# Filler products for TensorE: the unit matrix times itself in front of waits of a twelve-part decoder kernel

## The reference

```python
x = x + _L0_attn_ref(_layernorm(x), ...)       # first attention: 16 heads in pairs, p1 - lam * p2
x = x + _L0_xattn_ref(ctx_1024, _layernorm(x)) # warping: dynamic time warping against ctx
x = x + _L0_ffn_ref(_layernorm(x), ...)        # trees: 16 leaves, for q, k and v
x = x + _L1_attn_ref(_layernorm(x), ...)       # attention
x = x + _L1_xattn_ref(_layernorm(x), ctx, ...) # memory attention, gated
x = x + _L1_ffn_ref(_layernorm(x), ...)        # first mixture: shared expert + best 2 of 8
x = x + _L2_attn_ref(_layernorm(x), ...)       # pooling: running weighted sums
x = x + _L2_xattn_ref(_layernorm(x), ctx, ...) # attention to ctx
x = x + _L2_ffn_ref(_layernorm(x), ...)        # ternary weights
x = x + _L3_attn_ref(_layernorm(x), ...)       # attention with bias
x = x + _L3_xattn_ref(_layernorm(x), ctx, ...) # attention to ctx
x = x + _L3_ffn_ref(_layernorm(x), ...)        # second mixture: best 2 of 8, a limit per expert
```

```python
# first attention
attn = softmax(einsum('bhqd,bhkd->bhqk', q, k)).reshape(b, H, 2, n, n)
o = einsum('bhqk,bhkd->bhqd', attn[:, :, 0] - lam * attn[:, :, 1], v)
o = (o - mean(o)) * rsqrt(var(o) + 1e-5) * ln_g + ln_b      # per head
return o @ Wo
# memory attention
v_pool = concatenate([normed, memory], axis=1)
attn = softmax(where(mask, (normed @ q_w.T) @ (v_pool @ k_w.T).T * scale, -inf))
return (1 - alpha) * h + alpha * (attn @ v_pool)            # alpha = sigmoid(h @ gate_w.T + gate_b)
# pooling
qw = softmax((query @ Wqa + bqa) / sqrt(D)); pooled_query = cumsum(qw * query) / arange(1, S + 1)
mixed = pooled_query * keys
kw = softmax((mixed @ Wka + bka) / sqrt(D)); pooled_keys = cumsum(kw * mixed) / arange(1, S + 1)
return pooled_keys * values
# both mixtures: a token's two best experts, its place among the expert's tokens, and
y = gelu(x_of_expert @ w1[e] + b1[e]) @ w2[e] + b2[e]       # summed with the two gates
```

## Time and profile before

| | |
|---|---|
| median of 3 runs | 2319.32 us (2319.03 to 2327.06) |
| span of the profiled execution | 2356.9 us, 37.6 us (1.6%) above the median |
| TensorE busy in that span | 1774.8 us (75%), weight loads 1215.4 |
| VectorE, ScalarE, GpSimd busy | 1337.8 us (57%), 1099.5 (47%), 746.9 (32%) |
| first attention | 11.8 to 250.5 us, granted clock 0.85 in its loop (38.0 to 250.5) |
| memory attention | 908.2 to 1043.7 us, granted clock 0.81 |
| first mixture | 1045.8 to 1315.7 us, granted clock 0.91 |
| pooling | 1316.7 to 1453.1 us, granted clock 0.81 |
| second mixture | 2061.1 to 2351.2 us, granted clock 0.76 |

### The profile page before, as it was taken

How to read it: one execution, slowest core, us unless ns; L and a number is a source line. 1 busy time by engine, 2 the same in 40 slices (tenths; PEclk the granted TensorE clock), 3 DMA queues, 4 the chain that set the end, 5 groups by cost and what they waited for, 6 DMA issues and landing times. The chain is left out here.

```text
span 2356.9 us, 39525 instructions
## 1 busy us (share of the span) xinstructions
PE 1774.8 (75%) x14484; PEld 1215.4 (52%) x14484; DVE 1337.8 (57%) x3646; ACT 1099.5 (47%) x2273; POOL 746.9 (32%) x718
## 2 busy tenths in 40 slices
PE   3887553999895996767999386887788868743994
PEld 1555432435543664644798253565555535542774
DVE  3897587502123774654343365885369969862223
ACT  4775531223243775733344243774357657610441
POOL 1223201360354331146255002330223232165453
PEclk9888885798896998877999697998979969955997
DMA  4111361125623301102376200000000010011224
GB/s 158 83 83 82 104 235 45 49 75 150 161 70 132 124 2 50 37 30 85 110 238 201 75 1 27 28 20 10 3 1 2 2 37 28 11 49 60 62 81 138
DMA packets 145170, 173.18 MB, mean 73 GB/s; under 512 B 21073, under 2 KB 120593, under 8 KB 144049
## 3 DMA queue, kind: packets, MB, share of 16 engines
q1 hardware_dynamic: 125252, 129.09, 17.7%
q0 software_dynamic: 13248, 28.21, 3.6%
q10 hardware_dynamic: 6480, 13.37, 1.5%
HBM read 126.84 MB, written 79.05 MB: 87 GB/s over the span
## 5 line engine op out<-in xcount | busy, mean ns | idle before, releaser
L1154 PE MATMUL a_AV<-a_vx,a_pT 128*64 128x18 f32 (+1 forms) x3072 | 115.1, 224 | 33.0 <-DVE a_two L824 15.3
L1154 PEld LDWEIGHTS a_AV<-a_vx,a_pT 128*64 128x64 f32 x3072 | 105.9, 146 | 62.2 <-issue 28.6
L1016 ACT ACTIVATE a_e<-a_e 128x512 f32<-128x512 f32 x192 | 110.2, 622 | 58.7 <-DVE a_e L846 58.5
L1141 PE MATMUL a_TP<-ident,a_e 128*128 128x128 f32 x768 | 108.0, 285 | 20.0 <-ACT a_e L1016 19.4
L1021 ACT COPY a_pT<-a_TP 128x512 f32<-128x512 f32 x192 | 103.4, 588 | 39.6 <-PE a_TP L1141 39.4
L846 DVE TENSOR_TENSOR a_e<-a_S,a_mx 128x1024 f32<-128x1024 f32 x96 | 117.3, 1222 | 2.9
L1141 PEld LDWEIGHTS a_TP<-ident,a_e 128*128 128x128 f32 x768 | 89.2, 146 | 57.6 <-ACT a_e L1016 48.3
L1130 PE MATMUL a_S<-a_kbd,a_qT 64*64 64x512 f32 x768 | 113.8, 668 | 0.9 <-issue 0.6
L3620 POOL DMA_INDIRECT f_back<-f_ys,f_row x78 | 74.7, 957 | 97.5 <-DVE f_ys L3709 85.6
L3126 POOL DMA_INDIRECT f_back<-f_ys,f_row x80 | 76.6, 957 | 87.1 <-DVE f_ys L3287 66.9
L3759 ACT ACTIVATE f_h<-f_H,f_wt 128x256 f32<-128x256 f32 x156 | 65.2, 473 | 83.5 <-PE f_H L3835 83.5
(11 more groups left out here) (544 smaller groups left out, 4731.4 us busy)
## 6 DMA issues: line engine op xcount, KB each, us to landing
f_wt<-in_f_ew SPq DMA_DIRECT2D x39, 584.0 KB
f_slots<-in_blank SPq DMA_DIRECT2D x1, 18576.0 KB
f_wt<-in_f_leaf SPq DMA_DIRECT2D x94, 98.0 KB, 2.0
f_xs<-f_slots SPq DMA_DIRECT2D x47, 144.0 KB
memory_x_k<-w_stage ACTq DMA_DIRECT2D x24, 256.0 KB, 3.2
f_slots<-in_blank SPq DMA_DIRECT2D x1, 5760.0 KB
f_xs<-leaf_slots SPq DMA_DIRECT2D x22, 256.0 KB
leaf_out<-f_ys SPq DMA_DIRECT2D x22, 256.0 KB
```

The source lines that it names most:

```text
L1016: act.activation(eh, eh, ACT.Exp).then_inc(weights.sem, 1)
L1141: last = pe.transpose(TP[:, half, P * n:P * n + P], ev[:, 4 * half + n, :], k.ident[:, :])
L1154: last = pe.matmul(AV[64 * c:64 * c + 64, 2 * hp * W1:2 * (hp + 1) * W1], pT[:, hp, 64 * c:64 * c + 64], vx[:, g % 2, t, c, 2 * hp:2 * hp ...
```

## The change

A helper is added that multiplies the unit matrix (128 x 128, float32) by itself into a PSUM bank, n times, and its calls are put into TensorE's programs. No result of these products is read. 310 products are added: 8 x 4 in first attention, 8 x (5 + 5) in memory attention, 8 x 3 in pooling, 14 + 30 in the first mixture, 130 in the second (10 ahead of `turn_x(0)`, 5 behind it, and in each of the 8 batches 5 before `turn_x(b + 1)`, 5 behind it where there is one, and 5 behind `place(b)`). Nothing is removed. In first attention a wait comes with them: for the semaphore of the copy pT of tile i - 1, since TP is its bank.

```diff
+def keep_warm(pe, k, bank, n):
+
+    for _ in range(n):
+        pe.matmul(bank[:, 0:P], k.ident[:, :], k.ident[:, :], start=True, stop=True)
@@ first attention
                 early(g, t)
+                if i and t == 1 and diff:
+                    pe.wait_ge(pT_half.sem, 2 * (i - 1) + 1)
+                    keep_warm(pe, k, TP[:, 0, :], 4)
                 turn(i)
@@ memory attention
             def weigh(g):
                 if g:
                     pe.wait_ge(values_taken.sem, values_taken.after(g - 1))
+                keep_warm(pe, k, AV[:, 0, :], 5)
                 for t in range(GT):
...
                     weigh(i - 1)
+                if within(i - 1):
+                    keep_warm(pe, k, TP[:, 0, :], 5)
                 if within(i + 1):
                     project(i + 1)
@@ pooling
                     turn_q(i + 1)
+                    keep_warm(pe, k, QKV[:, 0, :], 3)
                 if within(i - 1):
                     total(i - 1, 1, C, (tail_ready.sem, tail_ready.after(i - 2)) if i >= 2 else None)
@@ routed (second mixture; shared is False)
             pe.wait_ge(setup_in.sem, n_early)
+            idle = 0 if shared else 5
+            keep_warm(pe, k, H[:, 0, :], 2 * idle)
             turn_x(0)
+            keep_warm(pe, k, H[:, 0, :], idle)
             make_logits(0)
             if shared:
                 pe.wait_ge(late_in.sem, n_late)
             for b in range(NBAT):
+                keep_warm(pe, k, H[:, 0, :], idle)
                 if b + 1 < NBAT:
                     turn_x(b + 1)
+                    keep_warm(pe, k, H[:, 0, :], idle)
                 place(b)
+                keep_warm(pe, k, H[:, 0, :], idle)
@@ first mixture
                 do_shared(1)
                 yield_shared(1)
+                keep_warm(pe, k, H[:, 2, :], 14)
                 r.place(pe, 2)
                 turn_batch(3)
                 r.make_logits(pe, 3)
                 do_shared(2)
                 yield_shared(2)
+                keep_warm(pe, k, H[:, 2, :], 30)
                 r.place(pe, 3)
```

## The result

The changed kernel takes 2329.34 us (median of 12 runs, 2320.45 to 2332.47), the kernel before 2321.36 (12 runs, 2312.0 to 2327.06). The ratio is 1.0033, 95% interval 1.0018 to 1.0048: slower by 8 us, beyond noise and less than the 0.5% that I took as what a measurement can tell. 2320.2 was forecast, with 2305 to 2334.

The account below looks back on a forecast made before the run. VectorE was taken to bound first attention, a TensorE-ScalarE chain memory attention, TensorE the first mixture, GpSimd the second while routing; half clock slows stretches. -2.7 - 1.0 - 5.4 + 9.0 + 1.0 = +0.9, so 2320.2 us, range 2305 to 2334.

Parts of the forecast that it names:

- first attention: Four products fit into TensorE's 1.37 us wait for ScalarE; -2.7 us, bounds nothing to -5.3.
- memory attention: First five products before the eight hold the clock, second five before `project` partly cost; net -1.0 us, bounds -5.6 to +8.9.
- pooling: Three products fit 0.67 us of idle time and four steps return to 12.46 us; -5.4 us, bounds 0 to -8.
- first mixture: The 44 products lie in TensorE's chain, 9.8 us, less 0.9 for a clock fall; +9.0 us, bounds -4 to +9.8.
- second mixture: First ten products start `turn_x(0)` 3.3 us late, faster work follows, GpSimd hides later ones; +1.0 us, bounds 0 to +6.
- the 0.9: First mixture: time lost in one 3.4 us fall of the clock, given back if the products keep it away.
- the 9.34 us wait: First mixture: a TensorE wait before the experts' start, doubted; if real, it hides the thirty products.
- Rival A: Whole kernel: clock held in every stretch and the wait of 9.34 us real; about -14 us, 2305; chance 0.22.
- the stall: First attention: VectorE waits 1.13 and later 0.39 us on TensorE's slow stretch; the 1.13 goes if the clock stays up.
- the 0.39: First attention: VectorE's later wait, the only part of the stall gained, seven times, 2.7 us.
- C: Whole kernel: transposes don't count as a busy TensorE, so the full clock does not engage; 2330 us; chance 0.12.
- B: Whole kernel: too few products to keep the clock, so they only cost; about +16 us, 2335; chance 0.14.

Follow-up runs that it names:

- e8: The kernel before plus only the first mixture's products, twice as many (28 + 60): 2339.44 us, ratio 1.0061 to the kernel before.
- e5: The kernel before plus only memory attention's 80 products: 2320.74 us against 2323.62, ratio 0.9988.
- e2: The kernel before plus only the first mixture's 44 products (14 + 30): 2371.57 us, ratio 1.0022 to the kernel before.
- e3: The changed kernel without the first mixture's 44 products: 2359.96 us, ratio 0.9972 to the kernel before.
- e7: The kernel before plus only first attention's 32 products, with their wait: 2322.41 us, ratio 0.9988 to the kernel before.
- e10: The changed kernel run again with no edit, in the third group: 2355.36 us, ratio 1.0008 to the kernel before.
- e11: Probe, one execution: GpSimd's power in first attention on 8 of 32 columns, other product counts varied; a first attention group takes 23.51 us.

## Why the prediction held, and where its terms were off

The sum was forecast as +0.9 and came out as +8.0 (+4 to +11). Gains and costs cancel in part, as forecast, and the mechanisms were right in most parts, but all five terms err the same way: three gains are too large and two costs too small. The result stands in the range because the range was wide enough for it, not because the terms were well sized. On the level without remote waits (pooling over all levels):

| part | forecast | measured, from stretches of the profiles |
|---|---|---|
| first attention | -2.7 | 0 |
| memory attention | -1.0 | 0 |
| pooling | -5.4 | -3.3 |
| first mixture | +9.0 | +11.5 |
| second mixture | +1.0 | +2.3 |
| sum | +0.9 | +10.5, and +8.0 timed |

**First mixture.** That 44 products lie in TensorE's chain was right (none, 44 and 88: 84.6, 96.1, 106.0). The term's error is the 0.9 that I let them give back by keeping the clock up. They don't: behind the fourteen the clock falls for 6.8 us in the changed kernel, and from `place(2)` to the shared expert's next second layer it takes 11.7 us there and in e8, against 10.0 in e5, which has no fall there. Behind the thirty it falls too in the changed kernel (5.43 against 3.84, 1.6 lost), but not behind the sixty of e8. Against that the changed kernel is 1.7 us faster than e5 ahead of all these products, where they can have no part. So 1.7 us of the excess are a fall that the products bring, seen in both profiles that have them and in none of the three without; the rest is the chance place of others. My doubt of the 9.34 us wait was wrong in its reason and right in its effect: it is real at some levels, absent at the level that was measured. Rival A's term (the 30 hidden in it) was not met even where the wait is real: e2 costs 1.4 to 9.0 us, where A has -2 for this part.

**Pooling.** The step was right in each part: three products in 0.67 us of idle time, and steps of 12.46. Over the seven steps even the size was right: 5.3 in the mean against 5.4. What the sum lacks is the stretch behind the last step, which then runs at half clock throughout (16.7 us against 14.4 to 14.8) in four of five kernels. 3.3 are left. How far this is a fall moved there by the products and how far chance is read from these profiles and not tested.

**First attention.** Right: VectorE's wait for GpSimd takes the place of most of the stall, 1.35 us in the two groups of the changed kernel that hold the clock, where 1.39 was forecast. A group gains 0.2 to 1.0 us (23.68 against 23.9 to 24.6). The power starts at 129.66 and so not ahead of TensorE's slow stretch, which begins at 124.89; what holds is that it starts ahead of VectorE's first wait for TensorE. But that the clock must stay up for it is not so: where it falls for 3.4 us in place of 6.8 (e3, e7, e10), the wait is 0.4 to 1.1 us and the group takes the same 23.68. Wrong: that the 0.39 is gained "seven times". I took each group to gain on its own and forgot that the last three run differently. There the changed kernel loses it again: this is e10, and then e5, which has no products there, at the same transposes of a_att:

```profile
206.60:210.00 3.40, 3.38 (x16) 3.40 (x17) 3.25 (x6) 1.91 (x4) 0.00 (x0) 0.50 0.20 87
```

```profile
208.15:211.60 3.45, 3.45 (x50) 3.10 (x50) 3.35 (x7) 1.81 (x4) 0.00 (x0) 1.00 0.20 85
```

The clock falls once more with products (0.50) and not without them (1.00), in a stretch with two waits ahead of it in both. That the fall's moved place costs the gain is read from these two and not tested by itself. What the four products do change is the length of a fall: in e10 3.4 us in four groups, where e5 has 6.8. The step that failed first, though, is that a gain here is a gain of the kernel: TensorE's wait for w_ctx behind this part takes it in (e7).

**Memory attention.** Right that the first five hold the clock for the eight products (in the changed kernel one step is slow, where the profile before has five; the sum priced three) and that the second five push the projection by 1.1. The net of nothing instead of -1.0 is inside the spread of one part between executions (127.0 to 130.1). On the third level, one profile each, first fives alone take 132.1 us, second fives alone 134.6, both 135.4 and none 135.1: by this the second fives give back what the first gain. Three of these four have a remote wait of 5.9 to 6.5 us in the part and the one with second fives alone has none, so it may well be worse than it looks.

**Second mixture.** The start was mis-sized: `turn_x(0)` is 4.5 us late where I had 3.3, since its products start 4.15 us into the part (2036.05), where I had put the transfer's end at 3.1; their own length, 4.4 us up to `turn_x(0)`, was right (4.3 forecast). What comes back behind that is 2.1 us, as forecast (2.5 less 0.4; 3.3 late would so have made 1.2, which the sum took as 1.0). GpSimd's period stayed, as forecast.

**The rivals.** By the number alone C's 2330 is the nearest to 2329.34, and the forecast's 2320.2 is not, so the rows have to decide. B (too few products to hold the clock) is right for some groups of first attention and wrong for pooling's steps and memory attention. C (transposes don't count) would have left the clock falling in memory attention, where transposes and five products stand ahead of the eight; in the changed kernel it fell in one step only. The Trainium skill, "TensorE: Matmul & The Clock Gate", Part 4 (PE-mode transpose), from which C came, is not borne out by that, as it isn't by the earlier trace rows; no run tested it by itself. The range held the result; A did not occur.

## What to carry to other kernels

Filler work for TensorE pays only in front of a wait that it doesn't lengthen: look for idle time that is longer than the products, and leave them out where the engine starts with none. The version with only such products beat both kernels (ratio 0.9952), the full set did not. Follow a fall that is gone to where the clock falls next: in pooling 2 of 5.3 us came back behind the last step. And before a freed stall is counted, look at who else waits on the same path: here GpSimd's power took over most of VectorE's wait, and the next part's wait for its input would have taken any rest.

## What the runs showed of the hardware

The kernel before had medians of 2321, 2369, 2324 and 2353 us in the four groups of runs. The profiles of the first and third of these show no wait that ends as remote, for any engine. In the others they add up to 74 to 160 us over ScalarE, VectorE and GpSimd, and so in the profile before (134.5). Most of them stand in the trees part (302 to 308 us against 314 to 332) and in the first mixture (254 against 265 to 278, without products), and one of about 6.5 us in memory attention in most, so that a level shows in which parts are long. What is behind remote is open; no run here tells it.

The granted clock did not follow the number of products alone: with the same four in each group of first attention it fell in some groups for 6.8 us, in others for 3.4 or not at all, in one execution (e10).

GpSimd's power over 128x32 values takes 5.43 us and over 128x8 1.64 (e7, e11).
